# Where one buffer of 8224 bytes lies: exp's buffer laid out behind aT_hi and aT_lo instead of in front of them

## The reference

```python
xn = layernorm(x)
q  = (xn @ Wq.T + bq)                   # 8 of the 32 heads are used, 128 numbers each
s  = elu(q) + 1
a  = s / (einsum(s, z) + 1e-6)          # one denominator for each row and head
out = x + (a @ M per head, repeated for the 4 heads of a group) @ Wo.T
        + xn @ (w * w_scale) + b        # w is int8
```

## Time and profile before

| | |
|---|---|
| median of 3 runs | 246.52 us (246.44 to 246.63) |
| profiled execution: its time | 246.23 us |
| profiled execution: its span | 244.4 us |
| TensorE busy | 236.9 us, 97% |
| VectorE busy | 176.0 us, 72% |
| ScalarE busy | 119.8 us, 49% |
| GpSimd busy | 113.5 us, 46% |
| chain that ended last | TensorE 83%, VectorE 7%, ScalarE 5% |

### The profile page before, as it was taken

The page is one execution under the profiler, slowest core; times in us unless marked ns, Lnnn a source line. Parts: engine busy times, 40 slices in busy tenths (PEclk is TensorE's granted clock), DMA queues, the critical chain, the costliest instruction groups (busy, mean ns, idle before and its releaser), DMA issues.

```text
span 244.4 us, 3386 instructions
## 1 busy us (share of the span) xinstructions
PE 236.9 (97%) x1030; PEld 186.6 (76%) x1030; DVE 176.0 (72%) x261; ACT 119.8 (49%) x276; POOL 113.5 (46%) x113
## 2 busy tenths in 40 slices
PE   6899899999999899999999999999999999999995
PEld 2477688887777578888888888888888888788885
DVE  3839995988998739978587594958666678983331
ACT  3663545629639824655463526346463747341110
POOL 2694743755272615563615326263404629667400
PEclk9999999999999999999999999999999999999999
DMA  6999999999270111424251525222122223245441
GB/s 237 405 415 408 396 232 216 215 216 210 71 247 14 49 48 50 129 54 123 53 168 49 168 52 168 60 80 83 34 53 70 54 75 107 76 134 146 114 169 51
DMA packets 21842, 34.83 MB, mean 142 GB/s; under 512 B 5185, under 2 KB 13121, under 8 KB 20673
## 3 DMA queue, kind: packets, MB, share of 16 engines
q1 hardware_dynamic: 19200, 26.63, 33.0%
q0 software_dynamic: 1376, 6.82, 13.3%
q10 hardware_dynamic: 1248, 1.18, 1.6%
HBM read 22.02 MB, written 4.19 MB: 107 GB/s over the span
## 4 chain that ended last, share of the span: by engine, by line
PE 83%; DVE 7%; ACT 5%; issue 2%; DMA 1%; DVEq 0%; ACTq 0%
PE attn_ps L787 13%; PE attn_ps L789 13%; PE attn_ps L788 13%; PE q_ps L787 9%; PE q_ps L789 9%; PE q_ps L788 9%; PE dense_ps L789 5%; PE dense_ps L787 5%; PE dense_ps L788 5%; ACT s L447 2%; PE attn_ps L851 2%; DMA x<-in_x 1%; DVE stats L557 1%; DVE wd_lo L612 1%; DVE q_ps L626 1%
## 5 line engine op out<-in xcount | busy, mean ns | idle before, releaser
L314 POOL TENSOR_TENSOR e_and_sz<-s,z_b 128x512 f32<-128x512 f32 x32 | 41.7, 1330 | 40.6 <-DVE den L638 40.4
L447 ACT ACTIVATE s<-s,rden 128x128 f32<-128x128 f32 x128 | 39.2, 389 | 40.4 <-DVE rden L642 40.4
L787 PE MATMUL attn_ps<-P_hi,aT_hi 128*128 128x512 f32 (+1 forms) x128 | 50.3, 393 | 0.9 <-DVE P_lo L617 0.8
L789 PE MATMUL attn_ps<-P_hi,aT_lo 128*128 128x512 f32 (+1 forms) x128 | 49.7, 388 | 0.0
L788 PE MATMUL attn_ps<-P_lo,aT_hi 128*128 128x512 f32 (+1 forms) x128 | 49.7, 388 | 0.0
L787 PE MATMUL q_ps<-WqT_hi,xT_hi 128*128 128x512 f32 x104 | 42.2, 406 | 0.9 <-DVE s L633 0.6
L789 PE MATMUL q_ps<-WqT_hi,xT_lo 128*128 128x512 f32 x104 | 40.6, 390 | 0.0
L788 PE MATMUL q_ps<-WqT_lo,xT_hi 128*128 128x512 f32 x104 | 40.5, 390 | 0.0
L284 POOL TENSOR_TENSOR xT<-xT,mean_b 128x512 f32<-128x512 f32 x14 | 20.0, 1431 | 38.4 <-ACT mean_b L396 36.0
L626 DVE SCALAR_TENSOR_TENSOR q_ps<-q_ps,rstd,bq_b 128x512 f32<-128x512 f32 x28 | 21.0, 753 | 20.6 <-PE q_ps L789 20.6
L787 PEld LDWEIGHTS attn_ps<-P_hi,aT_hi 128*128 128x128 f32 x128 | 24.0, 188 | 7.4 <-DVE P_lo L617 1.2
(11 more groups left out here) (82 smaller groups left out, 366.0 us busy)
## 6 DMA issues: line engine op xcount, KB each, us to landing
x<-in_WoT POOLq DMA_DIRECT2D x6, 1024.0 KB, 10.2
x<-in_x SPq DMA_DIRECT2D x16, 256.0 KB, 5.0
xT<-in_xT SPq DMA_DIRECT2D x16, 256.0 KB, 5.1
aT<-s SPq DMA_DIRECT2D x124, 32.0 KB, 1.8
out<-x SPq DMA_DIRECT2D x15, 256.0 KB, 2.3
MT<-s SPq DMA_DIRECT2D x96, 32.0 KB, 1.9
x<-in_WoT SPq DMA_DIRECT2D x2, 1024.0 KB, 14.0
s<-in_WqT SPq DMA_DIRECT2D x3, 512.0 KB, 6.7
```

The lines of the kernel that those rows point to most:

```text
L314: nc.gpsimd.tensor_tensor(sz_eps[:, :, h * D // 2:(h + 1) * D // 2].rearrange("p g (j c) -> p j g c", j=2), by_quarter(sbuf_s[:, t % SRING ...
L447: last = nc.scalar.activation(a_g, a_g, ACT.Copy, scale=rden[:, t % 2, g:g + 1])
L787: nc.tensor.matmul(out, x_hi, w_hi, start=start, stop=False)
L789: return nc.tensor.matmul(out, x_lo, w_hi, start=False, stop=stop)
```

## The change

The line that takes `e_and_sz` is moved down by four lines. Its length is 4 x (1024 + 8 x 129) = 8224 bytes in each partition. `aT_hi` (8192 bytes), `aT_lo` (8192), `mean_b` (1024) and `ident` (512) thereby begin 8224 bytes lower, `e_and_sz` begins 17,920 bytes higher, and every other tile stays where it was. In the built program aT_hi begins at byte 207,008 of a partition before and at 198,784 after; aT_lo at 215,200 and 206,976; e_and_sz at 198,784 and 216,704. No instruction is added, removed or moved on any engine.

```diff
         b_b = sb("b_b", [P, HID])
         sbuf_s = sb("s", [P, SRING, E])
         aT = sb("aT", [P, 4, E // 4])
-        e_and_sz = sb("e_and_sz", [P, E + G * (D + 1)])
         aT_hi = sb("aT_hi", [P, 2, G, P], F32R)
         aT_lo = sb("aT_lo", [P, 2, G, P], F32R)
         mean_b = sb("mean_b", [P, 2, P])
         ident = sb("ident", [P, P])
+        e_and_sz = sb("e_and_sz", [P, E + G * (D + 1)])
         neg_half = sb("neg_half", [P, 1])
         stats = sb("stats", [P, 2, 6])
         meanvar = sb("meanvar", [P, T, 2])
```

## The result

The changed kernel takes 244.98 us at the median of 10 runs (244.7 to 246.22), the one before 246.39 in 10 runs on the same chips (246.12 to 247.03). The ratio is 0.9952, with a 95% interval of 0.9935 to 0.997: 1.41 us less, where 1.65 was predicted. The profiled execution took 244.95 us (before 246.23), its span is 243.2.

What follows compares the result with a forecast made beforehand. TensorE was taken to bound the kernel, through the distance between matmul starts. Savings of 0.92 + 0.09 + 0.48 + 0.16 = 1.65 us from 246.52 gave 244.9 us, with a range for 8 in 10 of 244.0 to 245.8.

Steps and rivals of the forecast that it cites:

- What bounds the loop: Loop from 83 us: TensorE, busy 97% of the span; time is number of matmuls times the distance between their starts.
- The reason for the 6.6 ns: Attention matmuls: 233.3 ns against 226.7 because aT_hi and aT_lo start 32 bytes past a multiple of 64.
- slower: Attention: weights at 198,784 meet the moving stream of P at the same place of a line; +1.0 us, 247.5; chance 0.04.
- The change doesn't do it: Attention: the 6.6 ns come from something else in its operands, or 32 bytes don't matter; 246.5 us; chance 0.11.
- Terms 1 to 3: Attention products 0 to 10: -0.77 and -0.15, so product 11 starts 0.92 us earlier; 0.47 more goes into its wait.
- Term 4: Tail: product 11 saves 0.09 us, products 12 to 14 save 0.48, with the margin ahead of product 14 staying open.
- Term 5: Product 15, 48 matmuls of 256 columns: the wide ones' ratio of 2.8% saves 0.16 us.
- The first two rivals: Tail: its chain isn't in the way, 244.1 to 244.4 us (0.13); it takes back more, 245.3 to 245.8 (0.10).
- second rival: Tail takes back more: slower aT_lo around product 11, or a chain hanging on GpSimd or DMA; 245.3 to 245.8; chance 0.10.

Runs made afterwards that it cites:

- the mixed kernel: The changed kernel with 32 bytes of padding in front of aT_hi and 32 behind it; one execution, 247.27 us.
- run 236: Not a run label: in the changed kernel, product 14's first matmuls run 236, 228, 233 and 230 ns apart.

## Why the prediction was right, point by point

**What bounds the loop: right.** Time in the loop is matmuls times the distance between starts. The 6.6 ns that attention had over q and dense went away whole, in every product but the narrow product 15.

**The reason for the 6.6 ns: wrong as a rule, right for this change.** The prediction's step "What differs is where the stationary operand lies" took a start "32 bytes past a multiple of 64" for the cause. Two kernels with starts at multiples of 64 and of 128 stayed at 232 to 233, and one with every operand 32 past a multiple of 64 ran at 227. What the runs show is a dependence on the distance between weights and streamed operand (for attention the mean over products 12 to 14, for 0 and 160 that of q):

| distance mod 256 | 0 | 32 | 64 | 96 | 128 | 160 |
|---|---|---|---|---|---|---|
| ns for one of 512 columns | 226.7 | 233.3 | 233.3 | 234.3 | 232.4 | 233.3 |

In the trace of before both rules fit, since all other pairs had a distance of 0 as well as starts at multiples of 64; the one trace couldn't part them. Against the rival "slower" the prediction says that q and dense read aligned weights "at many relative places"; that was misread, for all of those are multiples of 256 bytes apart, and there lay the clue. The change sets both right at once, and that the number came out is luck as far as the rule goes. The 244.9 us came closer to the 244.98 measured than the saving did, because the kernel before had 246.39 here and not 246.52. A padding to the next multiple of 64, which the rule would have advised, brings nothing.

The distance is not the whole of it. Off 0 the matmuls don't come evenly: read to the nanosecond, the intervals between their starts alternate between 232 and 235 in the kernel before and between 231 and 236 with 32 bytes in front of aT_hi, and the mixed kernel fell below both its parts, to 231.1. At distance 0 they are 226 and 227, but for the first few of a product that comes behind a mean or a stop, and those of product 14 named below. What makes the pattern, no run here shows.

**The rivals.** "Slower" had a sound relation, the place of the weights as seen from the moving stream, and the opposite sign: meeting at the same place is the fast case. "The change doesn't do it" fell with product 7 at 5.44 us. By the Trainium skill, page "SBUF — State Buffer", section "Who interferes with whom", TensorE reads its two operands through independent ports. By that nothing would have changed; the measurement is against it, 226.7 to 233.3 ns for the same instructions at other addresses, and decides.

**Terms 1 to 3: right.** From attention(0) to product 11 the saving is 0.96 us for 0.92. The step lasts 13.75, the stop grew from 0.24 to 0.70 as predicted, the list of waits names aT_lo. The chain behind it is only partly as told: it did move forward as a whole, but its ScalarE link could be taken out without a gain. What holds it is VectorE's queue, with halves of aT_lo for products 10 and 11 that take 1.0 to 1.8 us beside GpSimd's work where 0.68 would do: with the addition out of the way the second half for product 10 took 0.68 instead of 1.78, and the stop ahead of product 11 was gone.

**Term 4: right in size, by less margin.** Product 11 saved 0.11 for 0.09, products 12 to 14 0.46 for 0.48. The room ahead of product 14 shrank to 0.3 us (ready at 228.88, started at 229.18), where 0.39 remained by the prediction's sum, because its aT_lo fell beside two additions. Product 14's first matmuls run 236, 228, 233 and 230 ns apart, not 226.7, though no wait is listed there.

**Term 5: wrong sign.** The prediction carried the 2.8% of the wide matmuls over to those of 256 columns. They went from 118.2 to 119.8 ns, +0.08 us for -0.16. In every kernel at distance 0 they take 119.8 or 119.9; at 32 they take 118.2, at 64 117.8, at 96 118.7 and at 128 120.1. This 0.24 us is the whole shortfall of the profiled pair: 1.65 - 0.24, with 0.04 more from the other terms, is 1.45 us.

**The first two rivals.** The tail neither let the 0.47 us through nor took more. The prediction's second rival took 1.585 us as the worst half of aT_lo, but that row holds only those made from `aT`; one made from `MT` took 1.78 in the same trace. That a shift parts aT_lo from GpSimd's additions was named as a chance; here it pushed the pair of product 14 together, within the margin. The run with the additions held back, the copy moved and the DMA issues first shows what parting them is worth: 0.9 us.

## What to carry to other kernels

Where TensorE is the bound, take the distance between matmul starts for each product and compare; if equal shapes differ by a few per cent, compare the byte addresses of weights and streamed operand in the built program, modulo 256, and test with a padding tile before moving anything. One trace in which two rules fit is not evidence for the handier one: a padding of 32 bytes told them apart. In this tail the elementwise step that feeds the bound engine must not lie beside a row of GpSimd instructions; a wait kept them apart, where moving them in the list only moved the meeting.

## What the runs showed of the hardware

- A float32 product's pass of 512 columns takes 226.7 ns from start to start, 544 clocks at the 2.4 GHz that the granted clock of 1.0 means, when the weights lie a multiple of 256 bytes from the streamed operand, and 232 to 234 ns, up to 562 clocks, at the distances 32, 64, 96, 128 and 160. Moving all tiles up together by 32 or 64 bytes changes nothing. Why, no run here shows; other distances weren't tried, and two distances mixed gave 231.1.
- At 256 columns distance 0 is not the fast case: 119.8 to 119.9 ns there, 118.2 at 32, 117.8 at 64, 118.7 at 96, 120.1 at 128.
- A VectorE instruction with two SBUF inputs is held up by GpSimd's: half a pair of aT_lo took 0.68 us alone, up to 1.8 beside one addition, 2.09 beside two and 3.42 beside three in a row. In these last two cases, and in the 1.57 of the run with the copy moved, it ended 0.56 us after the end of the last addition. By the Trainium skill, page "SBUF — State Buffer", section "Who interferes with whom", a VectorE instruction with two SBUF inputs contends with a GpSimd instruction that reads SBUF. The trace agrees, and shows that a row of additions holds it up for its whole length, though it began before the second and the third.
- Kernels that are alike up to there reach the first attention product at 85.6 to 86.9 us, the same kernel at 85.62 and 85.83. What decides that stays open.
